# Three fp32r products of high and low parts in place of fp32 products, for the feed-forward block's Pf, H and Y3

## The reference, cut to what matters

```
P = jnp.einsum('bsd,dr->bsr', x, U1)                      # 256 -> 64
H = jax.nn.gelu(jnp.einsum('bsr,rf->bsf', P, V1) + b1)    # 64 -> 1024
Q = jnp.einsum('bsf,fr->bsr', H, U2)                      # 1024 -> 64
return jnp.einsum('bsr,rd->bsd', Q, V2) + b2              # 64 -> 256
```

## Time and profile before

| | us |
|---|---|
| time, median of 3 runs (lowest to highest) | 1018.14 (1017.26 to 1018.73) |
| profiled execution, its own time | 1019.17 |
| its span | 1017.4 |
| busy PE / PEld / ACT / DVE / POOL | 981.4 / 787.0 / 580.7 / 502.9 / 205.7 |
| granted TensorE clock, mean | 0.995 |

### The profile page before, as it was taken

One profiled execution on the slowest core, in us unless ns is written; L12 is line 12 of the kernel. 1 busy time (PEld: TensorE's weight loads), 2 busy tenths in 40 slices (PEclk: granted clock), 3 DMA queues, 4 the chain that ended last, 5 costly groups with the idle time before them and its releaser, 6 DMA issues.

```text
span 1017.4 us, 21353 instructions
## 1 busy us (share of the span) xinstructions
PE 981.4 (96%) x8328; PEld 787.0 (77%) x8328; DVE 502.9 (49%) x1156; ACT 580.7 (57%) x1387; POOL 205.7 (20%) x356
## 2 busy tenths in 40 slices
PE   4999999999999999999999999999999999999997
PEld 3668787787878878787777878877787878877775
DVE  4444555463645546354554735545373554536252
ACT  3445457476574746657475665747467573755431
POOL 0010303031130312113030220403122040212130
PEclk9999999999999999999999999999999999999999
DMA  8222222222222221322222223222222222122000
GB/s 298 89 91 84 86 83 68 78 69 71 84 78 77 85 77 46 95 85 78 76 86 57 66 78 93 86 76 71 70 67 77 94 63 88 58 67 74 6 6 21
DMA packets 58002, 78.90 MB, mean 78 GB/s; under 512 B 10288, under 2 KB 39856, under 8 KB 57904
## 3 DMA queue, kind: packets, MB, share of 16 engines
q1 hardware_dynamic: 56192, 76.38, 24.3%
q10 hardware_dynamic: 1712, 1.16, 0.4%
HBM read 73.05 MB, written 4.46 MB: 76 GB/s over the span
## 4 chain that ended last, share of the span: by engine, by line
PE 66%; DVE 14%; ACT 13%; issue 4%; POOL 2%; SPq 1%; DMA 1%; POOLq 0%; DVEq 0%
PE gb L331 12%; PE scores L388 8%; PE scores L391 6%; PE gb L450 6%; PE gb L510 5%; PE acc L417 5%; PE ptp L400 4%; PE acc L413 4%; DVE inv L864 3%; PE acc L418 3%; ACT probs L624 3%; PE gb L559 3%; DVE probs L774 2%; ACT hid L693 2%; DVE nmax L767 2%
## 5 line engine op out<-in xcount | busy, mean ns | idle before, releaser
L624 ACT ACTIVATE probs<-scores,nmax 128x257 f32<-128x257 f32 x256 | 119.2, 471 | 172.4 <-DVE nmax L767 172.2
L767 DVE TENSOR_REDUCE nmax<-scores 128x2 f32<-128x514 f32 x128 | 88.5, 692 | 210.8 <-PE scores L391 210.8
L961 POOL TENSOR_TENSOR ptm<-probs,head 128x32 f32<-128x32 f32 x128 | 33.1, 259 | 593.7 <-DVE probs L774 593.7
L388 PE MATMUL scores<-raw_t,qk 128*128 128x257 f32 x512 | 133.2, 383 | 1.4 <-ACT qk L664 1.3
L388 PEld LDWEIGHTS scores<-raw_t,qk 128*128 128x128 f32 x512 | 87.8, 192 | 9.0 <-issue 1.7
L774 DVE TENSOR_TENSOR probs<-probs,rinv 128x514 f32<-128x514 f32 x128 | 89.0, 695 | 4.4
L391 PE MATMUL scores<-raw_t,qk 64*128 64x257 f32 x512 | 90.7, 431 | 0.0
L417 PE MATMUL acc<-pt,raw_n 128*128 128x256 f32 x256 | 90.0, 433 | 0.0
L413 PEld LDWEIGHTS acc<-pt,raw_n 128*64 128x64 f32 x1024 | 55.7, 137 | 42.8 <-issue 24.1
L400 PE MATMUL ptp<-ident,probs 128*128 128x128 f32 x512 | 78.7, 276 | 10.1 <-DVE probs L774 8.7
L413 PE MATMUL acc<-pt,raw_n 128*64 128x128 f32 x1024 | 83.2, 284 | 5.1 <-ACT pt L629 5.1
(11 more groups left out here) (145 smaller groups left out, 2318.7 us busy)
## 6 DMA issues: line engine op xcount, KB each, us to landing
raw_t<-in_ctx_t SPq DMA_DIRECT2D x128, 258.0 KB, 2.9
raw_n<-in_ctx_n SPq DMA_DIRECT2D x128, 192.0 KB, 2.4
xb<-in_x SPq DMA_DIRECT2D x16, 256.0 KB, 2.7
vsp<-tail_values SPq DMA_DIRECT2D x256, 2.0 KB
out<-ob SPq DMA_DIRECT2D x16, 256.0 KB, 2.2
xin<-in_x SPq DMA_DIRECT2D x15, 256.0 KB, 2.8
khat<-in_wq ACTq DMA_DIRECT2D x1, 512.0 KB, 4.5
wv<-in_wv SPq DMA_DIRECT2D x1, 512.0 KB, 6.1
```

The lines of the kernel that those rows point to most:

```text
L388: mm(scores[:, r, 0:L], w[:, b, r * P:(r + 1) * P], x[:, 0, 0:L], start=True, stop=False)
L624: go(probs[n % 2][:, r, 0:L], scores[:, r, 0:L], ACT.Exp, bias=nmax[:, r:r + 1], accum_out=rsum[:, r:r + 1]).then_inc(s["exp_ready"], 1)
L767: v_.tensor_reduce(nmax[:], scores[:, :, 0:L], AX.X, ALU.max, negate=True)\
```

## The change: what it does

Pf, H0 to H3 and Y3 become three fp32r products each: Pf and Y3 by `terms`, H by a loop over the three pairs of parts, with the row halves in turn. ACT writes `xt3_h`, `pf_h` and `qf_h` in fp32r; DVE writes `xt3_l`, `pf_l` and `qf_l` from PSUM and then drains the bank. The weights `u1`, `v1` and `v2` are divided once, on DVE in slot 3 of stage 0. For room, `xn2` is the buffer `xn1` (with waits for the transposes that read it), the raw weights are loaded into `s2` and `ke`, and the zeroing of `s2` moves behind the division. In stage 16 Qf goes ahead of WV. The products L587 read `wv_w` instead of `v1`.

```diff
-ENDING = {(NG, 0): [("Sq", OLD), ("WV", NEXT), ("Qf", OLDER)], (NG, 1): [("O2", OLD), ("Y3", OLDER), ("Y1", NEXT)],
+ENDING = {(NG, 0): [("Sq", OLD), ("Qf", OLDER), ("WV", NEXT)], (NG, 1): [("O2", OLD), ("Y3", OLDER), ("Y1", NEXT)],
...
-        xn2, xt3 = sb("xn2", [P, 2, D]), sb("xt3", [P, 2, T])
-        pf, qf = sb("pf", [P, T]), sb("qf", [P, T])
+        xn2 = xn1
+        xt3_h, xt3_l = (sb(n, [P, 2, T], F32R) for n in ("xt3_h", "xt3_l"))
+        pf_h, pf_l, qf_h, qf_l = (sb(n, [P, T], F32R) for n in ("pf_h", "pf_l", "qf_h", "qf_l"))
...
+        v1_raw = s2[:].rearrange("p t q -> p (t q)")
+        u1_raw, v2_raw = ke[:, 0:256], ke[:, 256:512]
...
-                for c in range(2):
-                    last = mm(out_[:, 0], u1[:, c], xt3[:, c], start=c == 0, stop=c == 1)
+                if g == 0:
+                    pe.wait_ge(s["v1_ready"], 1)
+                last = terms(out_[:, 0], [((u1_h[:, c], u1_l[:, c]), (xt3_h[:, c], xt3_l[:, c])) for c in range(2)])
...
-                    last_even = mm(even[:, c], v1[0:64, f:f + P], pf[0:64], start=True, stop=True)
-                    last_odd = mm(odd[:, c], v1[64:128, f + P:f + 2 * P], pf[64:128], start=True, stop=True)
+                    for k, (w, x) in enumerate(((v1_h, pf_h), (v1_l, pf_h), (v1_h, pf_l))):
+                        last_even = mm(even[:, c], w[0:64, f:f + P], x[0:64], start=k == 0, stop=k == 2)
+                        last_odd = mm(odd[:, c], w[64:128, f + P:f + 2 * P], x[64:128], start=k == 0, stop=k == 2)
...
-                    last = mm(out_[:, t], qf[:, t * P:(t + 1) * P], v2[:], start=True, stop=True)
+                    t_ = slice(t * P, (t + 1) * P)
+                    last = terms(out_[:, t], [((qf_h[:, t_], qf_l[:, t_]), (v2_h[:], v2_l[:]))])
...
-                        drain(n, g, go(pf[:], t[:, 0], ACT.Copy))
+                        go(pf_h[:], t[:, 0], ACT.Copy).then_inc(s["pf_h_ready"], 1)
...
                 elif n == "xn2":
+                    bank, k = BANK["XT2", min(g + 1, NG - 1)]
+                    dve.wait_ge(bank_filled[bank], k)
                     norm_apply(x12[g % 2], 2, g, xn2)
+                elif n in ("XT3", "Pf", "Qf"):
+                    t = wait_tile(n, g)
+                    t = t[:] if n == "XT3" else t[:, 0]
+                    hi, lo, ready = {"XT3": (xt3_h, xt3_l, "xt3_h_ready"), "Pf": (pf_h, pf_l, "pf_h_ready"),
+                                     "Qf": (qf_h, qf_l, "qf_h_ready")}[n]
+                    dve.wait_ge(s[ready], g + 1)
+                    drain(n, g, v_.tensor_tensor(lo[:], t, hi[:].bitcast(F32), ALU.subtract))
...
-            GAPS = [[["psp-1"], [], ["S2-2", "S3-2", "WV0-1", "WV1-1"]],
+            GAPS = [[["psp-1"], [], ["S2-2", "S3-2", "Qf-3", "WV0-1", "WV1-1"]],
...
-                    [[], ["su-1"], ["i0-1", "i1-1", "i2-1", "ti-1"]],
+                    [["XT3-2"], ["su-1"], ["i0-1", "i1-1", "i2-1", "ti-1", "Pf-2"]],
...
-                v_.memset(s2[:], 0.0)
...
+                    if (i, b) == (0, 3):
+                        split(u1_raw, *(x[:].rearrange("p c r -> p (c r)") for x in (u1_h, u1_l)))
+                        split(v2_raw, v2_h[:], v2_l[:])
+                        split(v1_raw, v1_h[:], v1_l[:], s["v1_ready"])
+                        dve.wait_ge(s["v1_ready"], 1)
+                        v_.memset(s2[:], 0.0)
```

More of the change, by code:

```diff
@@ L143, in build @@
         wo2_h, wo2_l = (sb(n, [P, 2, D], F32R) for n in ("wo2_h", "wo2_l"))
-        u1, u2 = sb("u1", [P, 2, 2 * R]), sb("u2", [P, 8, R])
-        v1, v2 = sb("v1", [P, F]), sb("v2", [P, D])
+        u2 = sb("u2", [P, 8, R])
+        u1_h, u1_l = (sb(n, [P, 2, 2 * R], F32R) for n in ("u1_h", "u1_l"))
+        v1_h, v1_l = (sb(n, [P, F], F32R) for n in ("v1_h", "v1_l"))
+        v2_h, v2_l = (sb(n, [P, D], F32R) for n in ("v2_h", "v2_l"))
         bo, b2 = sb("bo", [P, D]), sb("b2", [P, D])
@@ L221, in build @@
                  "acc_ready pc_ready ptm_ready var0_ready var1_ready var2_ready rstd0_ready rstd1_ready rstd2_ready xn0_ready xn1_ready xn2_ready xb_ready ob_ready "
-                 "wq_ready weights_ready wz_h_ready xt1_h_ready xt2_h_ready xt2_l_ready o_h_ready o2_h_ready tanh_ready dec_ready hat_ready dve_chain").split()
+                 "wq_ready v1_ready xt3_h_ready pf_h_ready qf_h_ready weights_ready wz_h_ready xt1_h_ready xt2_h_ready xt2_l_ready o_h_ready o2_h_ready tanh_ready dec_ready hat_ready dve_chain").split()
         s = {n: sem(n) for n in names}
@@ L234, in build @@
                    (wxt_raw, a["wxt"]), (ww_raw, a["ww"]), (w2_raw[:, 0:512], a["wk2"].rearrange("p c d -> p (c d)")), (w2_raw[:, 512:1024], a["wv2"].rearrange("p c d -> p (c d)")),
-                   (w2_raw[:, 1024:1536], a["wr2"].rearrange("p c d -> p (c d)")), (wo2_raw, a["wo2"].rearrange("p c d -> p (c d)")), (u1[:], a["u1"]), (v1[:], a["v1"]),
-                   (u2[:], a["u2"]), (v2[:], a["v2"]), (b2[:], a["b2"])]
+                   (w2_raw[:, 1024:1536], a["wr2"].rearrange("p c d -> p (c d)")), (wo2_raw, a["wo2"].rearrange("p c d -> p (c d)")), (u1_raw, a["u1"].rearrange("p c r -> p (c r)")), (v1_raw, a["v1"]),
+                   (u2[:], a["u2"]), (v2_raw, a["v2"]), (b2[:], a["b2"])]
         W_S, W_B = 16 * len(SMALL), 16 * len(WEIGHTS)
@@ L586, in stay_busy @@
                 for k in range(count):
-                    mm(scores[:, 0, 0:256], ident[:], v1[:, 0:256], start=True, stop=True)
+                    mm(scores[:, 0, 0:256], ident[:], wv_w[:, 0, 0:4].rearrange("p h d -> p (h d)"), start=True, stop=True)
             pe.wait_ge(id_in, 16)
@@ L653, in step @@
                     elif n == "XT3":
-                        drain(n, g, go(xt3[:], t[:], ACT.Copy))
+                        go(xt3_h[:], t[:], ACT.Copy).then_inc(s["xt3_h_ready"], 1)
                     elif n[0] == "q":
@@ L695, in step @@
                     elif n == "Qf":
-                        drain(n, g, go(qf[:], t[:, 0], ACT.Copy))
+                        go(qf_h[:], t[:, 0], ACT.Copy).then_inc(s["qf_h_ready"], 1)
             act.dma_start(wq_raw, a["wq"].rearrange("p c d -> p (c d)")).then_inc(wq_in, 16)
@@ L800, in step @@
                 elif n == "xn1":
+                    if g > 1:
+                        bank, k = BANK["XT3", g - 2]
+                        dve.wait_ge(bank_filled[bank], k)
                     norm_apply(x12[g % 2], 1, g, xn1)
                 elif n == "xn2":
+                    bank, k = BANK["XT2", min(g + 1, NG - 1)]
+                    dve.wait_ge(bank_filled[bank], k)
                     norm_apply(x12[g % 2], 2, g, xn2)
+                elif n in ("XT3", "Pf", "Qf"):
[5 more added lines that the diff above has]
+                    drain(n, g, v_.tensor_tensor(lo[:], t, hi[:].bitcast(F32), ALU.subtract))
                 elif n == "XT":
@@ L888, in _ @@
                     [[], [], ["S0-1", "S1-1"]]]
+            AT_END = ["Qf-3", "S2-2", "S3-2"]
             def gap(i, b, k):
-                for item in GAPS[b][k]:
+                for item in AT_END if (i, b, k) == (NG + 1, 0, 2) else GAPS[b][k]:
                     n, g = item[:-2], i + int(item[-2:])
```

## The result

| us | before | after |
|---|---|---|
| time, median of 4 runs (lowest to highest) | 1018.43 (1017.26 to 1018.77) | 1029.51 (1026.92 to 1032.83) |
| ratio, with its 95% interval | | 1.0111 (1.0083 to 1.0140) |
| profiled execution: its span | 1017.4 | 1030.1 |
| a steady stage | 59.88 | 59.97 |
| granted TensorE clock, mean | 0.995 | 0.988 |

A forecast was written before the change was run, and what follows sets the result against it. PE bounds each stage except a DVE and ACT chain from slot 4's scores to slot 7's start. Steady stages +0.3, start +0.5 and end +3.95 make +4.8 us on 1018.14, so 1023 us, range 1017 to 1028.

The forecast's parts named there:

- Qf's delay: Stage 16: Qf waits for the gelus behind the late H0, and the decay products stand behind Qf: +2.5 us.
- its rival: End: the clock falls over Qf and the decay products after PE idles ahead of H0: +2 to +4 us, chance 0.18.
- Chain, and which savings count: Slots 4 to 7: DVE and ACT bind, `pf_l` costs 0.35, only H2 and Y3 save 0.30: +0.05 a stage.
- The rival "faster": Steady stages: the chain does not bind and all four pieces save 0.60 a stage: 1014 us, chance 0.10.
- Row halves: H products: loads into different halves do not hinder each other, 0.119 us a pair; H0 and H2 save 0.15 each.
- The rival in which they take turns: H products: fp32r row halves alternate, so H2 takes 1.43 us instead of 0.71: +11, 1034 us, chance 0.07.
- `xt3_l` hidden: Ahead of slot 4's `nmax`: it fits DVE's idle time with 0.1 us to spare: 0, upper bound 0.15.
- Start: Stage 0: dividing the weights on DVE behind slot 3's `probs` makes slot 4's late: +0.5 us, which stays.
- WV's order: Stage 16, slot 0: WV runs behind Qf, and Y1 needs its low parts: +0.3 us (0 to 0.5).
- H0 in stage 16: Slot 4: `xt3_l` ahead of `su` and `pf_l` behind all reciprocals make H0 start 2.7 us late.
- The last chain: Last group's ACT to PE handovers: three subtractions add 1.8 us, faster products give back 0.45: +1.3.
- The range of the forecast: Whole kernel: 1020.4 to 1025.5 us; pairs at 0.106 give -1.7, `pf_l` at 0.41 and `xt3_l` at 0.15 give +2.5.

The follow-up runs named there:

- e1: Changed kernel with the DVE statistics of a coming group moved from ahead of slot 5's nmax to behind cf: 1014.44 us.
- e9: e1's kernel with H0 to H3 back as fp32 products, on the high parts alone: 1017.75 us.
- e6: Kernel before the change, with only the statistics moved behind cf: 1014.01 us.
- e5: Changed kernel with the old order in stage 16, slot 0 (WV ahead of Qf) put back: 1029.29 us.
- e7: e1's kernel with DVE's order in stage 16, slot 4 changed to su, xt3_l, i0, pf_l, i1, i2, ti: 1014.65 us.
- e11: e1's kernel with Qf's low part ahead of S0, S1, rhat early, stage 16's slot 4 reordered and the weights' division moved to slots 4, 6, 7: 1008.90 us.
- e8: e1's kernel with Qf's low part ahead of S0, S1 on DVE in stage 16, slot 7: 1011.86 us.
- e0: Changed kernel run again with no edit: 1029.79 us.
- e10: Changed kernel with POOL making the two rhat products ahead of the last tail column in stage 15: 1024.31 us.
- e12: Kernel before the change, with the statistics behind cf and rhat early in stage 15: 1011.14 us.
- e2: Changed kernel with three matmuls that nothing reads ahead of the decay products in stage 15, slot 7: 1026.05 us.

## Why the prediction was wrong, step by step

Two steps failed. The sum has the decay products of group 15 late by Qf's delay alone (+2.5) and puts the wait for Qf's bank at nothing, without a reason: the runs show 1.34 us of wait and 2.6 in all up to Y2. And it leaves out the clock: its rival has it fall behind H0's wait, and what moved the time was the stretch at 951 us, 4.67 us in half of the runs. The rest of the sum held.

- **Chain, and which savings count: right.** Stage +0.05 forecast, +0.09 measured (`pf_l` 0.33 for 0.35). e1 frees the chain and wins 0.84 a stage; e9 shows H0 hidden and H2 paid. The rival "faster" is dead for the kernel as it was, and e6 shows what it would have been worth: 0.41 a stage.
- **Row halves: right.** 0.11 to 0.12 a pair. The rival in which they take turns is ruled out. Beside it, the prediction sets its 119 ns against a figure of the Trainium skill (TensorE: Matmul & The Clock Gate, "Back-to-back issue gap"); the page gives that formula for isolated matmuls, and the 119 are from a stream with a weight load for each product, so the two don't disagree.
- **`xt3_l` hidden: right.** It ends 0.07 ahead of slot 4's `nmax`, which starts 2.18 us after its slot's first transposes, before and after.
- **Start:** +0.5 forecast, +0.6 measured (slot 5 of stage 0 at 55.82 instead of 55.22). That it stays is wrong in part: slot 7 of stage 0 gives 0.4 of it back (4.97 us instead of 5.36).
- **WV's order, +0.3: wrong, 0** (e5).
- **H0 in stage 16: right**, 2.7 late, and the decay products behind it 2.5. But e7 and e11 show that the step was half of the story: the decay products wait for POOL behind the same reciprocals, so of H0's 2.0 that e7 wins it keeps 0.8.
- **The last chain: right**, +1.4 for +1.3.
- **The term that is missing: the bank.** For the low parts the prediction asked who waits for the data, and never who waits for the bank. `qf_l` drains Qf's bank behind two copies: 1.3 to 1.4 us, shown by e8. The half clock that follows, which begins earlier and lasts 6.8 us instead of 3.4, adds 1.3 more up to Y2; e8's profile, without the wait, has 6.8 us too and is still 0.9 over the kernel before up to Y2, so this part is not shown to come from the wait.
- **The clock: a pause of PE, then half clock, but in another place.** The rival put it behind H0's wait (+2 to +4, 0.18); there it costs 0.2 to 0.3 us (e0, e1). It struck ahead of that, at 951, where the profile before already had 3.4 us of half clock; I read the earlier trace rows, the second such stretch, and not the first. In the changed kernel it lasted either 3.4 or 13.7 us; e10 takes the pause away and with it 5.5 us of the median, 1.2 of them the pause.
- **Luck.** The lower pair of runs, 1027, lies inside the stated 1017 to 1028 and next to the rival's 1025 to 1027, and owes it to the bank, not to the rival's place. Where a median of four falls depends on how many runs have the long stretch.
- **The range of the forecast.** Its lower end, 1020.4, does not follow from the one term given for it (1022.9 - 1.7 = 1021.2).

The forecast of 4.8, less 0.3 (WV), plus 0.5 (start and stages came to 1.33 instead of 0.8), 1.3 for the bank, 1.3 for the clock behind it and 2.3 for the long low clock (4.67 in half of the runs) makes 9.9 of the measured 11.1.

What stays open: what decides how long the clock stays low, and what the change has to do with it. Without the pause it did not fall there (e10, e11, e12), but e1 and e9 have the pause and their profiles no low stretch behind it, the profile before had 3.4 us, the changed kernel 3.4 or 13.7. None of the 42 runs of the kernel before beside the experiments has a mean clock under 0.993, so none shows the long stretch; with the change, and the pause left in, it comes and goes. Whether the H products have a part in it is not shown: e9, which has them in fp32 again, still has runs at 1021.25 and 1022.38 us (0.990 and 0.988), of which there is no profile. The repairs of the tail (e8, e11) were taken one at a time only in part: what the order in stage 16 or the start is worth by itself is read from traces, not from a time of its own.

## What to carry to other kernels

When a low part or any second reader takes over the draining of a buffer, list who waits for the buffer as well as who waits for the data, and look at what stands ahead of the drainer in its engine's order. Faster products buy nothing where another engine's order holds the stage: moving 1.1 us of DVE work behind one `nmax` was worth 0.34 us a stage in the old kernel (4.9 in all) and 0.84 in the new one (11.4 up to stage 15's slot 7). Read each stretch at half clock in the profile before the change, not the last one alone: here the first, of 3.4 us, stood where the changed kernel lost 4.67 more. And look at single runs before comparing medians: where they fall into two heaps, a median of four says mostly how many fell into each.

## What the runs showed of the hardware

- Runs of one program can differ by 5 us, 1026.8 to 1027.6 or 1031.9 to 1033.0. The two that were profiled differ by one stretch at half clock, 3.4 us in the one and 13.7 in the other. While it lasted, PE was busy in every window; 32 products with 32 columns, in pairs, took 3.56 us for 1.90.
- A pause of PE of 1.1 us ahead of such products went before each of those stretches. Without it (e10) or with it filled (e2) the stretch was gone from the profile. It was not enough every time: e1's and e9's profiles have the pause and no stretch.
- Three fp32r products in each of two row halves follow one another every 0.11 to 0.12 us a pair, as full-array ones do (0.119).
